# A transformer block's seams: last scatters under the next loads, constants one by one, barriers without a drain, biases in pairs

## The reference, cut to what matters

```
x  -> FFN 1:     x + half of a gated mixture of 16 experts (each takes its 512 best tokens) and a shared FFN
   -> attention: x + Wo(gate * linear attention(rope(q), rope(k), v)), state carried over chunks of 64 tokens
   -> MoE:       x + sum over each token's top 2 of 8 experts (gelu(h W1 + b1) W2 + b2), capacity 1280
   -> FFN 2:     the same form as FFN 1, with the same weights
```

## Time and profile before

| | |
|---|---|
| median of 3 runs | 2471.45 us (2471.08 to 2472.17) |
| profiled execution | 2471.66 us, its span 2469.9 us |
| PE busy | 2270.3 us (92%) |
| DVE, ACT, POOL busy | 1662.2 (67%), 891.9 (36%), 876.2 us (35%) |
| one scatter on POOL, MoE stage (80) | 1.70 us |
| one gather on POOL, MoE stage (76) | 1.08 us |
| share of DMA engines in 40 slices | `5003445444443100031244444435103445445442` |

### The profile page before, as it was taken

One profiled execution on the slowest core, in us unless ns is written; L12 is line 12 of the kernel. 1 busy time (PEld: TensorE's weight loads), 2 busy tenths in 40 slices (PEclk: granted clock), 3 DMA queues, 4 the chain that ended last, 5 costly groups with the idle time before them and its releaser, 6 DMA issues. The chain is left out here.

```text
span 2469.9 us, 37981 instructions
## 1 busy us (share of the span) xinstructions
PE 2270.3 (92%) x13564; PEld 1972.7 (80%) x13564; DVE 1662.2 (67%) x3588; ACT 891.9 (36%) x1623; POOL 876.2 (35%) x902
## 2 busy tenths in 40 slices
PE   6998999999996899963899999995998999999997
PEld 5887888888885677761799999984887888888887
DVE  5775777777774666655566666654685777777775
ACT  5222333333332666510233333335221333333332
POOL 4201323333322677620244444444211223323232
PEclk9998999999998899955899999997997999999999
DMA  5003445444443100031244444435103445445442
GB/s 174 26 28 118 112 134 133 130 129 110 139 127 83 57 18 20 20 97 38 81 81 82 83 81 80 81 42 175 29 27 104 119 120 134 116 129 136 127 130 44
DMA packets 153848, 228.21 MB, mean 92 GB/s; under 512 B 32960, under 2 KB 104384, under 8 KB 153536
## 3 DMA queue, kind: packets, MB, share of 16 engines
q1 hardware_dynamic: 102832, 157.82, 20.2%
q0 software_dynamic: 39936, 55.93, 13.4%
q10 hardware_dynamic: 10896, 12.07, 1.4%
HBM read 171.36 MB, written 54.39 MB: 91 GB/s over the span
## 5 line engine op out<-in xcount | busy, mean ns | idle before, releaser
L1082 ACT ACTIVATE me_act_f<-me_in,me_bias 128x512 f32<-128x512 f32 (+1 forms) x192 | 119.1, 620 | 294.5 <-PE me_in L125 293.6
L1082 ACT ACTIVATE f1e_silu<-f1e_in,f1e_bias 128x512 f32<-128x512 f32 (+1 forms) x136 | 90.1, 663 | 341.1 <-PE f1e_in L125 293.0
L1082 ACT ACTIVATE f2e_silu<-f2e_in,f2e_bias 128x512 f32<-128x512 f32 (+1 forms) x136 | 90.1, 663 | 341.1 <-PE f2e_in L125 292.8
L123 PE MATMUL f2e_in<-f2e_xt_hi,f2e_w_hi 128*128 128x512 f32 (+1 forms) x544 | 208.7, 384 | 3.8 <-DVE f2e_xt_lo L1143 2.3
L123 PE MATMUL f1e_in<-f1e_xt_hi,f1e_w_hi 128*128 128x512 f32 (+1 forms) x544 | 208.5, 383 | 3.9 <-DVE f1e_xt_lo L1143 2.3
L125 PE MATMUL f2e_in<-f2e_xt_hi,f2e_w_lo 128*128 128x512 f32 (+1 forms) x544 | 207.9, 382 | 0.0
L125 PE MATMUL f1e_in<-f1e_xt_hi,f1e_w_lo 128*128 128x512 f32 (+1 forms) x544 | 207.9, 382 | 0.0
L124 PE MATMUL f2e_in<-f2e_xt_lo,f2e_w_hi 128*128 128x512 f32 (+1 forms) x544 | 207.4, 381 | 0.0
L124 PE MATMUL f1e_in<-f1e_xt_lo,f1e_w_hi 128*128 128x512 f32 (+1 forms) x544 | 207.4, 381 | 0.0
L123 PE MATMUL me_down<-me_w_hi,me_act_hi 128*128 128x256 f32 x640 | 182.8, 286 | 0.0
L124 PE MATMUL me_down<-me_w_lo,me_act_hi 128*128 128x256 f32 x640 | 179.7, 281 | 0.0
(11 more groups left out here) (447 smaller groups left out, 6988.8 us busy)
## 6 DMA issues: line engine op xcount, KB each, us to landing
f_raw<-in_ffn_w SPq DMA_DIRECT2D x256, 384.0 KB, 3.6
m_raw<-in_moe_w SPq DMA_DIRECT2D x64, 256.0 KB, 2.8
f1s_x_all<-in_x SPq DMA_DIRECT2D x8, 512.0 KB, 8.8
after_ffn<-f1s_out SPq DMA_DIRECT2D x8, 512.0 KB, 2.9
after_moe<-ma_x_all SPq DMA_DIRECT2D x32, 128.0 KB, 1.7
m_h<-mr_h SPq DMA_DIRECT2D x16, 256.0 KB, 2.2
f2s_x_all<-after_moe SPq DMA_DIRECT2D x8, 512.0 KB, 8.1
out<-f2s_out SPq DMA_DIRECT2D x8, 512.0 KB, 2.9
```

Of the source, the lines that this page charges most:

```text
L123: pe.matmul(out, lh, rh, start=first, stop=False, skip_group_check=True)
L1082: act.activation(dst[:, st % 2, 0:n], ps_in[st % 2][0][:, 0:n], func, bias=bias[:, b, f:f + 1]).then_inc(silu_done, 1)
```

## The change

- `Last`, made once around the whole program, holds a tile for the last two results of an expert stage and a semaphore per stage. The last expert's last two tiles go there, and their scatters are waited for by the next stage's SP before it loads x (or at the end of the program by POOL), no longer within the stage.
- `ffn_front` no longer waits for its last two stores; POOL of the expert stage does, before the first scatter. In a front that follows another stage, x's group 0 is loaded after ident and the gate weights.
- All blocks are opened with `no_gpsimd_drain=True`: POOL's DRAIN at the block's end goes, the other engines keep theirs.
- Attention's constants: scale, the weights' two halves and the bias have semaphores of their own; PE waits for the other five, POOL and DVE only in round 0. w_lo comes before, the bias's low part after the first statistics.
- In the MoE stage (all but the last expert) the biases are added in pairs of tiles, one pair after each of five consecutive activations.

```diff
+class Last:
+    def __init__(self, scope):
+        self.tiles, self.scope = scope.sb("tiles", [P, 4 * D]), scope
+        self.landed, self.asked = None, 0
+    def of_stage(self, tag):
+        self.landed, self.asked = self.scope.sem(f"{tag}_landed"), 0
+        return self.landed
+    def wait(self, eng):
+        if self.asked:
+            eng.wait_ge(self.landed, self.asked)
...
@@ ffn_front
-        block = s.enter_context(nc.Block())
+        block = s.enter_context(nc.Block(no_gpsimd_drain=True))
...
-            sp.dma_start(tiles(x_all, 0), rows_of(x_in, 0)).then_inc(x_in_s[0], 16)
+            if not last.asked:
+                sp.dma_start(tiles(x_all, 0), rows_of(x_in, 0)).then_inc(x_in_s[0], 16)
             sp.dma_start(ident[:], consts[:, C_IDENT:C_IDENT + P]).then_inc(ident_in, 16)
             sp.dma_start(gz, gate_w).then_inc(gz_in, 16)
-            for g in range(1, G):
+            last.wait(sp)
+            for g in range(0 if last.asked else 1, G):
...
             for u in range(2):
-                sp.wait_ge(out_stored[u], 16 * (G // 2))
+                sp.wait_ge(out_stored[u], 16 * (G // 2 - 1))
@@ run_experts
+        def is_last(e, j):
+            return e == E - 1 and j >= NT - 2
+        def out_tile(e, b, j):
+            return last_tiles[:, j - (NT - 2), :] if is_last(e, j) else out[:, b, j, :]
...
-                                        in_=out[:, b, j, :], in_offset=None, compute_op=ALU.add
-                                        ).then_inc(scattered, 16)
+                                        in_=out_tile(e, b, j), in_offset=None, compute_op=ALU.add
+                                        ).then_inc(last_landed if is_last(e, j) else scattered, 16)
...
+                if gated and e == 0:
+                    for u in range(2):
+                        pool.wait_ge(acc_stored[u], 16 * (T // GT // 2))
...
-                pool.wait_ge(scattered, e * (16 * NT) + 16 * NT)
+                pool.wait_ge(scattered, e * (16 * NT) + 16 * (NT if left else NT - 2))
...
             experts(one)
+            last.asked = 32
+            if ends_program:
+                last.wait(pool)
...
+            def add_chunk(e, st, b):
+                if ends_at(e, st) and in_chunks(e):
+                    c = at_step(e, st)[1]
+                    add_bias(e, b, c, range(*chunks(e)[c]))
+            def add_pair(e, p):
+                if not in_chunks(e):
+                    add_bias(e, e % 2, 2 * p // 4, range(2 * p, 2 * p + 2))
...
                     activate(e, st, b)
-                    if ends_at(e, st - LAG):
-                        add_bias(e, st - LAG, b)
+                    add_chunk(e, st - LAG, b)
+                    if st == steps(e) - 1:
+                        add_pair(e, 0)
+                    if e and LAG <= st < NI - 1:
+                        add_pair(e - 1, st + 1)
...
-                    if ends_at(e, steps(e) - LAG + st):
-                        add_bias(e, steps(e) - LAG + st, b)
+                    add_chunk(e, steps(e) - LAG + st, b)
+                    add_pair(e, st + 1)
@@ attention
+            last.wait(sp)
...
-            pool.wait_ge(const_in, 16 * N_CONST)
...
+                if r == 0:
+                    pool.wait_ge(const_in, 16 * N_CONST)
...
+            act.dma_start(scale[:], w["norm1"]).then_inc(scale_in, 16)
+            for k in range(K):
+                act.dma_start(w_raw[:, k], w["qkvg"][:, k]).then_inc(w_in[k], 16)
+            act.dma_start(bias[:], w["qkvg_b"].to_broadcast([P, 4 * D])).then_inc(bias_in, 16)
...
-            act.wait_ge(const_in, 16 * N_CONST)
+            act.wait_ge(scale_in, 16)
+            for k in range(K):
+                act.wait_ge(w_in[k], 16)
+                act.activation(w_hi[:, k], w_raw[:, k], ACT.Copy, scale=scale[:, k:k + 1]).then_inc(w_hi_done, 1)
+            act.wait_ge(bias_in, 16)
             act.copy(bias_rows[:], bias[:]).then_inc(rows_rounded, 1)
...
-            dve.wait_ge(const_in, 16 * N_CONST)
             weights_low()
             rounds([(6, divide), (5, state0), (0, stat), (4, feature), (3, rotate), (5, state1), (2, split_low),
-                    (6, add_out)])
+                    (6, add_out)], after_first=bias_low)
@@ macaron
+    with Scope(nc, "last") as s:
+        last = Last(s)
```

More of the change, by code:

```diff
@@ L90, in __init__ @@
         self.gid_done = scope.sem("gid_done")
+        self.stored = [scope.sem(f"stored{u}") for u in range(2)]
     def for_experts(self):
-        return self.ident, self.raw, self.rows, self.raw_in, self.rows_in
+        return self.ident, self.raw, self.rows, self.raw_in, self.rows_in, self.stored
+class Last:
[8 more added lines that the diff above has]
+            eng.wait_ge(self.landed, self.asked)
 class Chain:
@@ L228, in ffn_front @@
         h_out = [s.sem(f"h_out{u}") for u in range(H_RING)]
-        out_stored = [s.sem(f"out_stored{u}") for u in range(2)]
+        out_stored = first.stored
         gz_hi_done, gz_lo_done, w_hi_done, w_lo_done = (
@@ L863, in run_experts @@
 def run_experts(nc, tag, E, NT, gated, w_dram, bias_dram, down_bias, consts, h_rows, acc,
-                gather_ids, scatter_ids, first):
+                gather_ids, scatter_ids, first, last, ends_program):
     F_T = FFN_F // P
@@ L879, in run_experts @@
     AHEAD = 4
-    ident, raw, rows, raw_in, rows_in = first
+    ident, raw, rows, raw_in, rows_in, acc_stored = first
     LAG = 2
@@ L893, in run_experts @@
         out = s.sb("out", [P, 2, NT, D])
+        last_tiles, last_landed = last.tiles[:, 0:2 * D].rearrange("p (j d) -> p j d", d=D), last.of_stage(tag)
         gcol = s.sb("gcol", [P, 2, NT])
@@ L1101, in read_sums @@
                 for t in range(t0, t1):
-                    ins = act.activation(out[:, b, t, :], ps_down[:, t, :], ACT.Copy, scale=gcol[:, b, t:t + 1])
+                    ins = act.activation(out_tile(e, b, t), ps_down[:, t, :], ACT.Copy, scale=gcol[:, b, t:t + 1])
                 ins.then_inc(read_out, 1)
@@ L1229, in ffn, with attention @@
         first = First(s, FFN_E, NT, 2 * K * P + D)
-        ffn_front(nc, tag + "s", x_in, gate_w, shared_w, ffn_w, consts, h_rows, acc, ids, first)
+        ffn_front(nc, tag + "s", x_in, gate_w, shared_w, ffn_w, consts, h_rows, acc, ids, first, last)
         run_experts(nc, tag + "e", FFN_E, NT, True, ffn_w, ffn_b, ffn_db, consts, h_rows, acc, ids, ids,
-                    first.for_experts())
-def attention(nc, tag, x_in, acc, w, consts, x2_all, sums):
+                    first.for_experts(), last, ends_program)
+def attention(nc, tag, x_in, acc, w, consts, x2_all, sums, last):
     Q = T // BATCH
@@ L1304, in loaded, with rounds @@
             return x_in_s[i][r % 2]
-        def rounds(steps):
+        def rounds(steps, after_first=None):
             for n in range(T + max(lag for lag, _ in steps)):
+                if n == 1 and after_first:
+                    after_first()
                 for lag, step in steps:
@@ L1774, in attention_and_moe @@
             x2_all, sums = s2.sb("x2_all", [P, T, D]), s2.sb("sums", [P, T])
-            attention(nc, tag + "a", x_in, acc, w, consts, x2_all, sums)
+            attention(nc, tag + "a", x_in, acc, w, consts, x2_all, sums, last)
             route(nc, tag + "r", w, consts, x2_all, sums, h_rows, best, best_i, acc[N:N + MOE_CAP])
@@ L1779, in attention_and_moe @@
         run_experts(nc, tag + "e", MOE_E, NT, False, w["moe_w"], w["moe_b"], w["moe_db"], consts, h_rows, acc,
-                    ids, ids2, first.for_experts())
+                    ids, ids2, first.for_experts(), last, False)
 def macaron(nc, w, out):
```

48 lines of the change are left out of this document (25 added, 23 removed).

## The result

The changed kernel takes 2435.5 us (median of four executions, 2432.9 to 2438.6) against 2471.8 before: ratio 0.985, interval 0.983 to 0.987. The profiled execution took 2437.5 us with a span of 2435.7, 34.2 us less than the span before. A second set of executions, with the experiments, gave 2437.2 against 2472.1 (ratio 0.9856, 0.9841 to 0.9871): 35 us, and just inside the range.

A forecast was written before the change was run, and what follows sets the result against it. Within stages PE was taken to bound the kernel, leaving seams between stages and stops at expert changes. Terms 4.8 + 2.5 + 8.4 + 1.2 + 0.3 - 0.5 + 5.5 = 22.2 us off 2471.45 gave 2449, range 2437 to 2459.

The forecast's parts named there:

- the price: Time of POOL's block-end DRAIN after expert stages, 2.58, 3.97 and 2.58 us; forecast to move to line 77, not be saved.
- Rival 1: At the stage seams: the drain's price vanishes instead of moving to line 77; 33.6 us saved, 2438, chance 20%.
- attention's start: Seam from first experts to attention: first issue at 788.1 instead of 790.6, 2.5 us saved.
- the list stage: Seam from list stage to MoE experts: DRAIN waits for the gathers, only one barrier goes, 0.3 us saved.
- the third stage: Seam from MoE experts to the third stage: x load issued earlier, 1.2 us saved, ends 0.7 and 1.6.
- the end: Program's end: the wait stays, the DRAIN moves behind the barrier, a third clear with its barrier is added, 0.5 us lost.
- Fronts to experts: Two front-to-expert seams: SP no longer waits for the last two stores, 2.4 us each, 4.8 us saved.
- Attention's constants: Attention's start: constants waited for separately, PE's wait for the last five binds at 13.3 us; 8.4 us saved.
- the chain: Attention's start: weights landing, w_hi, w_lo, statistics, then PE's first transpose, 11.8 us after the first issue.
- Pairs: MoE expert changes: two biases instead of four ahead of the next activation, 5.5 us saved, ends 3 and 8.8.
- Rivals 2 to 4: 2: drain price paid in full after landing, 2458, 15%. 3: MoE weights late, 2479, 3%. 4: change ineffective, 2467, 2%.
- Rival 4: Another wait at attention's start (x's loads) takes the constants' 8.4 us, drains paid in full; 4.7 us remain, 2467, 2%.

## Why the prediction was wrong

**The step that failed** is this one: "Nothing in the rows distinguishes the two DRAINs but their order. So I take it that the price moves from the block's end (line 884) to line 77 and isn't saved." The kernel before with the drains alone left out is 10.5 to 12 us faster, and line 77's DRAINs stay short. Rival 1, held at 20%, had the mechanism, its size at each seam within 0.5 us (5.0 at attention, 4.8 into the third stage, 2.3 and 2.1) and nearly the time, 2438. What the rows did distinguish was the line: one belongs to the block, which the flag changes, the other to the clear. That they were the same instruction but for their order was an assumption, and the rows could not have shown otherwise.

**The signs were chosen badly too.** The prediction would have been borne out by a DRAIN of 2 to 4 us at line 77 after the expert stages, and the changed kernel shows two of 3.07. But their length is POOL's own last two scatters, which were still being issued; the price behind it is 0.1 us. The sign that tells is how long the DRAIN lasts after the engine's last operation, and at the program's end, where nothing is being issued, line 77 takes 0.05 to 0.07.

**It hit four terms at once:** attention's start 2.5 (5.0 measured), the list stage 0.3 (2.2), the third stage 1.2 (4.3), the end -0.5 (2.0). These 10.0 us are nine tenths of the 11.1 between forecast and trace. The rule that a drain waits only for an idle engine was weighed and put behind a row about the other kind of DRAIN. The end has a second, smaller miss: the third clear cost 0.9 us, not 0.5.

**Fronts to experts:** right, 4.8, and the DRAIN at line 77 cost 0.14 there.

**Attention's constants:** the size was right (8.4 against 8.9), the working only in part, and that they agree is in part luck. The forecast had the weights at 5.5 us after the first issue, the chain at 11.8 and PE's wait binding at 13.3. In the changed kernel the last constant came at 12.3, a microsecond sooner, and the chain at 12.85, a microsecond later. That microsecond is POOL's first step beside the bias's low part, which the forecast had put there as free. Alone the weights come at 8.0 and the edit brings 6.6; it brings 8.9 in the changed kernel since the landing of the scatters holds x's loads back. Rival 1 had this delay and gave it 0.5 us; it brings 2.2. PE's wait and the chain nearly tie: last constant 795.8, transpose 796.3.

**Pairs:** right. Stops of 0.67 us for "about 0.5", 4.8 to 5.3 us for the 5.5.

**Rivals 2 to 4:** none happened. No PE work waited for m_raw, and the granted clock of the MoE stage was 0.98, after 0.97. Rival 4 counts x's loads among the five constants that PE waits for; they aren't.

## What to carry to other kernels

A block's end on POOL cost 2.6 to 4 us by itself after 124 to 156 indirect DMAs, on an idle engine and with all landed, and 0.07 where there were none. If semaphores already say what has landed, open the block without that drain. Don't carry the price of one DRAIN to another line's: leave one out and look. Read a DRAIN from the end of the engine's last operation, not from its own start. A load that isn't needed yet is not free beside one that is: on the kernel before, holding x back until the weights had landed brought the transposes 2.2 us forward. On the changed kernel, where the landing already holds x back, more of it brought nothing that the times show.

## What the runs showed of the hardware that I had not expected

- The block end's DRAIN is paid once: 2.58 or 3.97 us, and a second one right behind 0.03 to 0.05. With no indirect DMA ahead it ends 0.07 us behind POOL's last operation. It starts counting when POOL is idle: it ended 2.7 and 4.7 us behind the end of the last scatter's issue, though that scatter lands 2.1 to 2.2 behind it.
- The clear's DRAIN ends 0.1 us behind the end of the scatter's issue, 2.2 us ahead of its landing.
- With x's loads issued at the same time, the second 512 KB half of the weights landed 8.0 us after the first issue (7.6 in the changed kernel with the drains back); with 1.2 us between them 5.6 and 6.1; with most of x held 6.4. Undivided and issued first, all 1024 KB landed in 5.1 beside the same loads of x.
- Two small steps of POOL took 1.61 and 1.20 us beside DVE's low parts, and 0.74 and 0.26 without.
